# Splitting the expert weights of layers 1 and 2 ahead, in layer 1's last run, and loading the parts in the routing

## The reference

```
# layer 1, graph: three runs over the adjacency, each a product, a relu, a layernorm
h1 = x @ W1 + b1
n1 = _layernorm(jax.nn.relu(A @ h1) + h1, g1, be1)
h2 = n1 @ W2 + b2
n2 = _layernorm(jax.nn.relu(A @ h2) + n1, g2, be2)
h3 = n2 @ W3 + b3
n3 = _layernorm(jax.nn.relu(A @ h3) + n2, g3, be3)
# layers 1 and 2, feed-forward: 8 experts (256 -> 512 -> 256), the best two of each row
top2_vals, top2_idx = jax.lax.top_k(probs, 2)
h = act(x @ W1[e] + b1[e]);  y = h @ W2[e] + b2[e]
```

## Time and profile before

| | |
|---|---|
| three runs, us | 2624.55, 2637.11, 2652.12; median 2637.11 |
| the profiled execution, us | 2658.08 |
| its span, us | 2655.9 |
| PE busy | 2075.8 us (78%) |
| DVE busy | 1573.1 us (59%) |
| ACT busy | 1082.8 us (41%) |
| POOL busy | 497.0 us (19%) |
| DMA | 357.69 MB, mean 135 GB/s |

### The profile page before, as it was taken

The page is one execution under the profiler, slowest core; times in us unless marked ns, Lnnn a source line. Parts: engine busy times, 40 slices in busy tenths (PEclk is TensorE's granted clock), DMA queues, the critical chain, the costliest instruction groups (busy, mean ns, idle before and its releaser), DMA issues. The chain is left out here.

```text
span 2655.9 us, 46982 instructions
## 1 busy us (share of the span) xinstructions
PE 2075.8 (78%) x17062; PEld 1393.9 (52%) x17062; DVE 1573.1 (59%) x2950; ACT 1082.8 (41%) x2336; POOL 497.0 (19%) x464
## 2 busy tenths in 40 slices
PE   5899284899999999358856899178954899997597
PEld 3688152588888888346643677166732222222243
DVE  4666654454545566753346897633364899996633
ACT  5454264421212233345534775445543123233344
POOL 0000453000000000374430233544410000000200
PEclk9899597699999999769988899599966999998689
DMA  4899368055455555332223673511230332321000
GB/s 134 256 357 303 103 142 240 15 199 237 198 239 201 238 234 235 109 110 65 65 89 105 168 184 84 160 57 61 67 106 34 125 112 78 90 77 51 16 0 42
DMA packets 211970, 357.69 MB, mean 135 GB/s; under 512 B 18680, under 2 KB 165753, under 8 KB 197050
## 3 DMA queue, kind: packets, MB, share of 16 engines
q1 hardware_dynamic: 189118, 310.39, 34.7%
q0 software_dynamic: 13152, 35.93, 5.2%
q10 hardware_dynamic: 9504, 8.65, 1.0%
HBM read 291.81 MB, written 63.12 MB: 134 GB/s over the span
## 5 line engine op out<-in xcount | busy, mean ns | idle before, releaser
L881 PE MATMUL ps<-R,BIG 128*128 128x256 f16 (+1 forms) x1936 | 532.5, 275 | 23.1 <-DVE BIG L1357 13.4
L882 PE MATMUL ps<-R,BIG 128*128 128x256 f16 x1936 | 528.7, 273 | 0.0
L883 PE MATMUL ps<-R,BIG 128*128 128x256 f16 (+1 forms) x1936 | 528.6, 273 | 0.0
L1799 DVE TENSOR_TENSOR X<-X 128x512 f16<-128x512 f32 (+1 forms) x152 | 84.4, 556 | 332.3 <-ACT X L1780 318.7
L2265 PE MATMUL ps<-BIG 128*64 128x452 f32 x1056 | 233.7, 564 | 35.2 <-DVE BIG L2380 30.8
L881 PEld LDWEIGHTS ps<-R,BIG 128*128 128x128 f16 x1936 | 187.9, 97 | 58.4 <-DVE BIG L1357 13.7
L260 PE MATMUL ps<-X,BIG 128*128 128x128 f16 x904 | 189.6, 227 | 25.3 <-issue 20.0
L882 PEld LDWEIGHTS ps<-R,BIG 128*128 128x128 f16 x1936 | 190.4, 98 | 23.2
L883 PEld LDWEIGHTS ps<-R,BIG 128*128 128x128 f16 x1936 | 188.3, 97 | 26.4
L262 PE MATMUL ps<-X,BIG 128*128 128x128 f16 x904 | 191.0, 227 | 6.6 <-issue 6.5
L261 PE MATMUL ps<-X,BIG 128*128 128x128 f16 x904 | 186.3, 222 | 11.5 <-issue 11.5
(11 more groups left out here) (347 smaller groups left out, 4599.7 us busy)
## 6 DMA issues: line engine op xcount, KB each, us to landing
BIG<-adj_split SPq DMA_DIRECT2D x66, 1408.0 KB, 12.8
BIG<-in_adjT SPq DMA_DIRECT2D x42, 1408.0 KB, 11.1
adj_split<-BIG SPq DMA_DIRECT2D x22, 1408.0 KB
BIG<-in_adj SPq DMA_DIRECT2D x22, 1408.0 KB, 6.1
BIG<-in_adjT SPq DMA_DIRECT2D x66, 452.0 KB, 3.3
BIG<-in_f SPq DMA_DIRECT2D x88, 256.0 KB, 3.0
BIG<-expert_out SPq DMA_DIRECT2D x44, 256.0 KB, 2.9
rows_split<-row ACTq DMA_DIRECT2D x66, 128.0 KB, 3.4
```

The source lines that it names most:

```text
L881: pe.matmul(out[:, 0:n], pr[:, 0, k, :], h[:, k, 0:n], start=start, stop=False)
L882: pe.matmul(out[:, 0:D], pr[:, 0, k, :], l[:, k, 0:D], start=False, stop=False)
L883: return pe.matmul(out[:, 0:n], pr[:, 1, k, :], h[:, k, 0:n], start=False, stop=stop)
```

## The change

The 64 blocks of the expert weights of layers 1 and 2 are now split in layer 1's third run instead of in the two routings. The tile XX, which is free in that run, holds four raw blocks and four pairs of parts. In turn n, SP stores the parts of group n-50 (four blocks) in a new tensor in memory, `experts_split`, and loads the raw blocks of group n-49. ACT makes four high parts at the end of its turn, and POOL the four low parts. The routing of layers 1 and 2 then issues eight loads of 1 MB each, and neither ACT nor POOL has anything to do with these weights there. The arithmetic is the same. Layer 0's expert weights and all graph weights stay as they were.

```
+        class FromMemory:
+            def __init__(self, i, hi, lo, n):
+                self.i, self.parts, self.n, self.done = i, (hi, lo), n, []
+            def sp(self, sp, sem):
+                for c in range(4):
+                    at = slice(c * self.n // 4, (c + 1) * self.n // 4)
+                    for h in range(2):
+                        sp.dma_start(self.parts[h][:, at], later[self.i - 1, h, :, at]).then_inc(sem, 16)
...
+        class LaterWeights:
+            N = 4 * E1 * H1 // ST
+            GROUPS = 2 * N // 4
+            raw = XX[:, 0:4 * ST].rearrange("p (u n) -> p u n", u=4)
+            cut = XX[:, 4 * ST:8 * ST].bitcast(F16).rearrange("p (u h n) -> p u h n", u=4, h=2)
...
+            def load(self, sp, g):
+                for b, m, i, at in self.group(g):
+                    sp.wait_ge(WS["lo"], m - 3)
+                    sp.dma_start(self.raw[:, b % 4, :], io[f"f{i + 1}"][:, at]).then_inc(WS[f"ld{m % 4}"], 16)
+            def store(self, sp, s, g):
+                for b, m, i, at in self.group(g):
+                    sp.wait_ge(WS["lo"], m + 1)
+                    sp.dma_start(later[i, :, :, at].rearrange("h p n -> p h n"), self.cut[:, b % 4, :, :])\
+                      .then_inc(s[f"w{b % 4}"], 16)
+            def high(self, act, s, g):
+                for b, m, i, at in self.group(g):
+                    act.wait_ge(WS[f"ld{m % 4}"], 16 * (m // 4) + 16)
+                    s.wait(act, f"w{b % 4}", 16 * g)
+                    act.activation(self.cut[:, b % 4, 0, :], self.raw[:, b % 4, :], ACT.Copy).then_inc(WS["hi"], 1)
+            def low(self, pool):
+                for g in range(self.GROUPS):
+                    for b, m, i, at in self.group(g):
+                        pool.wait_ge(WS["hi"], m + 1)
+                        pool.tensor_tensor(self.cut[:, b % 4, 1, :], self.raw[:, b % 4, :], self.cut[:, b % 4, 0, :], ALU.subtract)\
+                            .then_inc(WS["lo"], 1)
...
 # P1.sp, after the load of panel n
+                    g = n - 2 * KT - 5
+                    if 0 <= g - 1 < LATER.GROUPS:
+                        LATER.store(sp, s, g - 1)
+                    if 0 <= g < LATER.GROUPS:
+                        LATER.load(sp, g)
...
 # P1.act, the end of a turn of the third run
                         rows.high(act, s, t, 2 * KT)
+                    if 0 <= t - 1 < LATER.GROUPS:
+                        LATER.high(act, s, t - 1)
+            def pool(self, pool):
+                LATER.low(pool)
...
 # Route.sp
-                F[self.i].sp(sp)
+                if self.i:
+                    F[self.i].sp(sp, self.st["sel"])
+                else:
+                    F[0].sp(sp)
```

More of the change, by code:

```diff
@@ L177, in build @@
         ys_dram = nc.dram_tensor("expert_out", (2 * NP + P * JMAX, D), F32).ap()
+        later = nc.dram_tensor("experts_split", (2, 2, P, 4 * E1 * H1), F16).ap()
         DUMP = 2 * NP
@@ L351, in fsplit, with act @@
             return BIG[:, 0:n // 2].bitcast(F16), BIG[:, n // 2:n].bitcast(F16)
+        class FromMemory:
[6 more added lines that the diff above has]
+                        sp.dma_start(self.parts[h][:, at], later[self.i - 1, h, :, at]).then_inc(sem, 16)
+            def act(self, act, first=0, last=None):
+                pass
+            def pool(self, pool):
+                pass
@@ new lines, in build, with __init__, group @@
+        class LaterWeights:
[3 more added lines that the diff above has]
+            cut = XX[:, 4 * ST:8 * ST].bitcast(F16).rearrange("p (u h n) -> p u h n", u=4, h=2)
+            def __init__(self):
+                self.base = wblocks[0]
+                wblocks[0] += 2 * self.N
+            def group(self, g):
+                for u in range(4):
+                    b = 4 * g + u
+                    yield b, self.base + b, b // self.N, slice(b % self.N * ST, (b % self.N + 1) * ST)
+            def load(self, sp, g):
[18 more added lines that the diff above has]
+                            .then_inc(WS["lo"], 1)
@@ L353, in build @@
         NF = {0: 4 * E0 * H0, 1: 4 * E1 * H1, 2: 4 * E1 * H1}
         W = {0: Weights(io["w0"], WH, WLo, 4, WB)}
-        F = {}
-        for i in range(3):
-            F[i] = Weights(io[f"f{i}"], *fsplit(NF[i]), NF[i] // ST, ST)
+        F = {0: Weights(io["f0"], *fsplit(NF[0]), NF[0] // ST, ST)}
+        W[1] = Weights(io["w1"], WH, WLo, 4, WB)
+        LATER = LaterWeights()
+        for i in (1, 2):
+            F[i] = FromMemory(i, *fsplit(NF[i]), NF[i])
             W[i + 1] = Weights(io[f"w{i + 1}"], WH, WLo, 4, WB)
@@ L1067, in __init__ @@
                                 used=T3, e1=T3, ev=T3, ag=T3 + KT, le=T3 + KT, ny=2 * KT, xh=2 * KT, xl=2 * KT, mm=2 * KT,
-                                hh=2 * KT, hl=2 * KT, t=T3, dg=14, gm=4, gb=4, **Rows.totals())
+                                hh=2 * KT, hl=2 * KT, t=T3, **{f"w{u}": 16 * LATER.GROUPS for u in range(4)}, dg=14, gm=4, gb=4, **Rows.totals())
                 self.flow, self.free, self.kept = flow, free, kept
                 self.H = [(HAh, HAl), (HBh, HBl), (HAh, HAl)]
-                self.done = [self.st.end(n) for n in ("sr0", "sr1", "sr2", "lg")]
+                self.done = [self.st.end(n) for n in ("sr0", "sr1", "sr2", "lg", "w0", "w1", "w2", "w3")]
                 self.freed = [self.st.end("used"), self.st.end("rl"), self.st.end("cb")]
@@ L1390, in __init__ @@
                 self.st = Stage("route", lm=1, v=0, a={"argmax": 0, "softmax": 2, "top2": 2}[kind], mk=1, rk=1, oh=1, ix=1,
-                                cw=1, sel=16)
+                                cw=1, sel=16 if i == 0 else 16 * 9)
                 self.done = [self.st.end("cw"), self.st.end("sel")]
@@ L2629, in _ @@
             c0.pool(pool)
+            p1.pool(pool)
             many_rows.pool(pool)
```

## The result

| | before | after |
|---|---|---|
| median of four runs each, us | 2641.41 | 2668.14 |
| lowest and highest, us | 2624.55 to 2652.12 | 2664.44 to 2670.38 |
| profiled execution, us (span) | 2658.08 (2655.9) | 2664.44 (2662.5) |
| DMA, MB in all | 357.69 | 391.26 |
| DVE busy, us | 1573.1 | 1545.6 |

The ratio is 1.0093, with an interval of 1.0068 to 1.0118: slower by 25 us (18 to 31). That is just within the 1% (26 us) that the prediction called no change, and the interval reaches beyond it. 2649 was forecast, 2668 came; 4 of these 19 us are the median of before, which a fourth run raised from 2637 to 2641.

The account below looks back on a forecast made before the run. It took PE, with ACT and DVE as tight, to bound the third run and DVE's chain the routings. Terms -22.8 - 28.3 + 4 + 31 + 20 + 3 + 5 = +12 us on 2637.11 gave 2649 us; range 2617 to 2690.

Parts of the forecast that it names:

- routing, layer 1: Layer 1's routing: without POOL's subtractions the DVE chain loses its stretched steps, 8.5 and 14.3 us; -22.8 us.
- routing, layer 2: Layer 2's routing: stretched DVE steps lose 19.2 us and the wait for the exponential 9.1 us; -28.3 us.
- late start of both chains: Both routings: eight loads start beside the last row write the chain waits for; 2 us each, bounds 0 and 4; +4 us.
- third run, copies: Layer 1's third run: ACT's four copies lengthen each of 16 turns by 2.06 us, less 2 us of PE's slack; +31 us.
- third run, lock: Layer 1's third run: POOL's subtractions hold up DVE steps through the shared port, 1.25 us a turn; +20 us, bounds 0 and 27.
- third run, DMA: Layer 1's third run: 4.02 MB a turn at 355 GB/s nearly fills the queue; raw blocks sometimes late for ACT; +3 us.
- start of layer 1's experts: Layer 1's experts: POOL's 9.1 us set-up now follows the fourth gather and PE stands; +5 us, bounds 0 and 9.
- memory is the bound: Rival, third run: at 310 GB/s a turn takes 13.0 us instead of 8.4; +31 us in all, 2668 us; chance 0.14.
- Only the copies cost: Rival, third run: lock does not bite, memory keeps up, set-up is hidden; -20 us, 2617 us; chance 0.15.
- The routings don't shrink: Rival, routings: DVE's long steps come from something that stays, only 9.1 us won; +54 us, 2691 us; chance 0.05.
- The clock: Rival, third run: clock falls to 1.2 GHz and PE bounds at 14.7 us a panel; +59 us, 2696 us; chance 0.06.

Follow-up runs that it names:

- x8: Changed kernel with POOL's set-up run beside the routing and the loads of the parts issued behind the row's last write; ratio 1.0042 to the kernel before.
- x5: Changed kernel loading and storing only 64 of each 512 columns after the first group, copies and subtractions whole; ratio 1.0004 to the kernel before.
- x4: Changed kernel with POOL subtracting 8 columns of a block instead of 512, all but the first group; ratio 1.0061 to the kernel before.
- x9: Kernel before, with ACT splitting 6 weight blocks instead of 16 ahead of the exponential in layer 2's routing; ratio 0.9986 to the kernel before.
- x6: Changed kernel with ACT copying 8 of each 512 columns after the first group; loads, subtractions and stores whole; ratio 1.0087 to the kernel before.
- x1: The kernel before, unchanged, run again on another chip for a second profile; 2609.94 us.
- x11: Kernel before with adjacency blocks loaded and counted in the first two runs, not the third, and 6 blocks ahead in layer 2's routing; ratio 0.9882.
- x10: Changed kernel with adjacency blocks loaded and counted in every second turn of the first two runs, none in the third; ratio 0.9949 to the kernel before.

## Why the prediction was right or wrong

No change that can be told, with the wrong sign: that was right, and the size short by half: +12 us in the sum, +25 measured. It held by little, and in part by luck: the limit was 26 us, the misses on the bytes (+12.8) and the late start (+5.5) went one way, and mainly the lock (-4.5) went the other. The prediction's own terms against what the runs showed:

| term | predicted | measured | from |
|---|---|---|---|
| routing, layer 1 | -22.8 | -22.65 | chain 33.73 for 56.38 |
| routing, layer 2 | -28.3 | -28.3 | chain 32.7 for 61.0 |
| late start of both chains | +4 | +9.5 | waits after; x8 |
| third run, copies | +31 | +30 | x5, 45.3 less the lock |
| third run, lock | +20 | +15.5 | 16 x 0.97; x5 |
| third run, DMA | +3 | +15.8 | 61.15 less 45.3 (x5, an eighth of the bytes) |
| start of layer 1's experts | +5 | +4.3 | PE's wait; x8 |
| sum | +12 | +24 | ratio: +25 (18 to 31) |

*Right: the routings.* Both chains shrank by the sums worked out, to 0.2 us. Before the change ACT's copies were there as well, but x4 shows in the third run that the long steps go with POOL's work alone. The split of layer 2's 28.3 us into 9.1 for the wait and 19.2 for the steps is not borne out: taking the wait away alone shortens the chain by 3.2 (x9). The Trainium skill's rule of the exclusive lock (SBUF — State Buffer, Who interferes with whom) agrees with both places: the chains, 22.65 and 28.3 us, and the third run, 0.97 us a turn.

*Right in kind, too large: the lock.* The "two waits of half a subtraction each", 1.25 us a turn, are indeed two waits, but of 0.26 and 0.71 us.

*Wrong: "So the queue is nearly full: on average it fits", and +3 us for the run.* The working had 11.3 us of transfers beside 11.7 us of engine work, and both were off. A turn moves 4.18 MB (x6) and not 4.02, mostly because the row's own write of 128 KB was left out. At the 355 GB/s assumed that is 11.8 us, at x6's 350 it is 11.9. And the engine turn is 11.1 (x5), not 11.7. So the order of the two is turned round, and the bytes are the bound. The rate itself was no mistake: 341 GB/s was moved after the change at a share of 0.96, and 350 and 353 in x6 and x4 at 0.99 and 1.00.

The rival *memory is the bound* named this mechanism. Its threshold of 344 GB/s came from the same 4.02 MB and 11.7 us; with 4.18 MB and 11.1 us it is 377, and no stretch of the third run shown here is as fast. Its 2668 us meets the result by luck: its turns were 13.0 us, at 310 GB/s, where 12.2 came, and it lacked the 5.5 us of late starts. So it was the better description of the third run at a price that was too high, and it deserved more than 0.14: with both sides 4% apart, either could have been the bound.

*Wrong: half of the wait for the late start.* The bounds of 0 and 4 us a routing took the old wait as the measure. But the row's write now lies behind a burst of 8 MB issued ahead of it, and both waits grew by more than the 4 us (4.3 and 5.2); with the burst behind the write they don't grow (x8).

*The other rivals.* "Only the copies cost" falls by x5. "The routings don't shrink" falls by the two chains. The clock did fall, to 0.86 to 0.91 in the third run, but not to half; the relu stands right behind the copy, so PE is not the late one. The chance of 0.06 was not put to a test of its own.

What stays open: the execution traced of before spent some 18 us more behind its routings than the sum allows. It was itself 17 us above the median of the four, and x1 spent less there, but no run says why. And x5 ended 7 us lower than its parts.

## What to carry to other kernels

Before work with bytes goes into a tight loop, put all bytes of a turn, small writes too, over a rate measured at a full share, beside the engines' turn. Where the two lie as close as here (11.9 and 11.1 us), expect the larger and somewhat more (12.2), not that one hides the other. A burst of loads belongs behind the small write that the next stage waits for. And look at what else sits in the loop that is tight: moving the counts to turns in which DVE was idle, together with 6 blocks ahead in place of 16, won 31 us (x11, of which x9 alone has 4), where the change cost 25.

## What the runs showed of the hardware

- A burst on SP's queue delays a write of one row tile on ACT's queue. DVE waited for it 8.27 and 7.46 us with eight 1 MB loads issued ahead, 2.35 and 2.22 with the loads behind it (x8).
- Loads, stores and panels together moved 341 GB/s at a DMA share of 0.96 (after), 338 and 339 at 0.97 and 0.98 (x10), 350 at 0.99 (x6) and 353 at 1.00 (x4). So the 341 of after is not the most that this mix reaches.
- A POOL subtraction stretches short DVE steps beside it: in the third run 0.42 to 0.68 and 0.16 to 0.87 us, and with POOL thin they are 0.43 and 0.16 (x4).
- POOL's set-up ahead of its first subtraction after the maximum is paid where that instruction stands: 9.09 us, 7.39 behind the gathers, 7.00 beside the routing (x8). The Trainium skill (GPSIMD Engine Reference, Instruction dispatch) has about 6 us for the first call to code just loaded; all three rows are above it.
- When a queue stands behind an engine, taking work off the engine makes the wait for the queue longer: in x4 ACT's wait went from 2.70 to 4.07 us, and of the lock's 15.5 us only 6.8 were won.
